# Two causal masking routes, a bias fold in four steps, and a packed ring of exponentials

## The reference

```
xn1 = ln(x, g1, be1)
q, k, v = xn1 @ Wq_s + bq_s, xn1 @ Wk_s + bk_s, xn1 @ Wv_s + bv_s     # 16 heads of 32
scores = where(tril, q @ k.T * sqrt(32), -inf)                      # causal
x = x + softmax(scores) @ v @ W1 + b1
xn2 = ln(x, g2, be2)
x = x + softmax((xn2 @ Wq_c + bq_c) @ kc.T * sqrt(32)) @ vc @ W2 + b2    # over the context
x = x + relu(ln(x, g3, be3) @ Wf1 + bf1) @ Wf2 + bf2
```

## Time and profile before

| | |
|---|---|
| median of three runs | 2273.32 us |
| the profiled execution | 2272.72 us |
| its span | 2270.9 us |
| busy PE, PEld | 2161.4, 1604.5 us |
| busy DVE, ACT, POOL | 1395.7, 868.7, 932.4 us |
| scores of causal attention end | about 966 us into the span |

### The profile page before, as it was taken

How to read it: one execution, slowest core, us unless ns; L and a number is a source line. 1 busy time by engine, 2 the same in 40 slices (tenths; PEclk the granted TensorE clock), 3 DMA queues, 4 the chain that set the end, 5 groups by cost and what they waited for, 6 DMA issues and landing times.

```text
span 2270.9 us, 32174 instructions
## 1 busy us (share of the span) xinstructions
PE 2161.4 (95%) x11590; PEld 1604.5 (71%) x11590; DVE 1395.7 (61%) x3349; ACT 868.7 (38%) x1610; POOL 932.4 (41%) x943
## 2 busy tenths in 40 slices
PE   7999999999999998889999998999999999999996
PEld 5666666666656664467777776888887887888784
DVE  5577766876786676456666677543455636455546
ACT  4156555655565555534333433221221222121213
POOL 1068767777777778643333342101020202111112
PEclk9999999999999997999999999999999999999998
DMA  7655555555564564211122121320112121121101
GB/s 234 78 82 97 93 85 87 106 89 83 91 111 76 82 96 126 71 56 56 56 70 77 63 80 42 121 84 24 61 61 82 53 74 66 65 66 56 42 33 47
DMA packets 106324, 177.34 MB, mean 78 GB/s; under 512 B 18335, under 2 KB 23455, under 8 KB 106161
## 3 DMA queue, kind: packets, MB, share of 16 engines
q1 hardware_dynamic: 106164, 175.29, 33.1%
HBM read 83.67 MB, written 40.13 MB: 55 GB/s over the span
## 4 chain that ended last, share of the span: by engine, by line
PE 81%; DVE 7%; ACT 5%; issue 3%; POOL 2%; DMA 1%; SPq 0%; POOLq 0%; ACTq 0%; DVEq 0%
PE psum L55 19%; PE psum L56 18%; PE psum L57 18%; PE psum L821 6%; PE psum L766 6%; PE psum L809 5%; PE psum L724 1%; DVE psum L1027 1%; ACT sx L1377 1%; PE psum L830 1%; PE psum L743 1%; PE psum L1327 1%; DMA small<-es 1%; PE psum L1319 1%; PE psum L1268 1%
## 5 line engine op out<-in xcount | busy, mean ns | idle before, releaser
L681 POOL TENSOR_TENSOR es<-es,er 128x512 f32<-128x512 f32 (+3 forms) x640 | 588.0, 959 | 258.4 <-PE psum L821 243.6
L922 ACT ACTIVATE er<-psum 128x512 f32<-128x512 f32 (+3 forms) x640 | 278.4, 471 | 285.6 <-DVE psum L1038 176.2
L1027 DVE CUSTOM_DVE_ANT_0 psum<-psum,mask_ts 128x384 f32<-128x384 f32 (+3 forms) x512 | 249.4, 502 | 152.9 <-PE psum L766 150.6
L766 PE MATMUL psum<-ks,qs 96*128 96x512 f32 (+3 forms) x768 | 260.4, 371 | 7.4 <-DVE mx L1027 3.5
L809 PE MATMUL psum<-qs,ks 100*128 100x512 f32 (+3 forms) x768 | 252.0, 365 | 10.6 <-DVE mx L1027 5.1
L1876 ACT ACTIVATE fy<-psum,cols 128x512 f32<-128x512 f32 x128 | 88.2, 689 | 451.9 <-PE psum L57 451.4
L766 PEld LDWEIGHTS psum<-ks,qs 96*128 96x128 f32 x768 | 139.7, 191 | 115.2 <-issue 32.9
L1031 DVE TENSOR_REDUCE mx<-psum 128x1 fp32r<-128x512 f32 x256 | 175.6, 686 | 61.0 <-PE psum L766 60.0
L55 PE MATMUL psum<-fh,hh 128*128 128x512 f32 x512 | 201.0, 393 | 7.1 <-DVE hl L1977 7.1
L55 PE MATMUL psum<-fah,fh 128*128 128x512 f32 x512 | 202.9, 396 | 0.0
L1975 DVE CAST hh<-fy 128x512 fp32r<-128x512 f32 x128 | 61.2, 478 | 228.5 <-ACT fy L1876 228.1
(11 more groups left out here) (260 smaller groups left out, 4588.7 us busy)
## 6 DMA issues: line engine op xcount, KB each, us to landing
qs<-stage SPq DMA_DIRECT2D x96, 256.0 KB, 5.7
ks<-stage SPq DMA_DIRECT2D x96, 256.0 KB, 8.3
rs<-rs_d SPq DMA_DIRECT2D x32, 256.0 KB
sa_d<-rs SPq DMA_DIRECT2D x32, 256.0 KB, 2.1
sx<-sa_d SPq DMA_DIRECT2D x8, 1024.0 KB, 5.7
xt<-in_x SPq DMA_DIRECT2D x32, 256.0 KB, 6.0
x_d<-xt SPq DMA_DIRECT2D x32, 256.0 KB, 2.0
fw<-in_Wf SPq DMA_DIRECT2D x16, 512.0 KB, 5.3
```

The costliest lines, as they stand in the source:

```text
L681: e.tensor_tensor(es, es, er, ALU.add).then_inc(s_add.sem, 1)
L766: t = e.matmul(bank1(*s)[:, v * wd:v * wd + wd], Q.qs[par][0:96, i, 128 * ti:128 * ti + 128], Q.ks[par][0:96, i, c0:c0 + wd], start=True, ...
L922: e.activation(dst, bank1("sc", g, c2, j, i)[:, off:512], ACT.Exp, scale=SCALE).then_inc(s_freeS.sem, 1)
L1027: t = e.tensor_tensor_reduce(out=ps, in0=ps, in1=mask_ts[:, 512 - wd:512], scale=1.0, scalar=-3e38, op0=ALU.add, op1=ALU.max, accum_out=mx ...
```

## The change

Four things. The list of planned times is first rewritten as tables with a row for each of the first four, the middle eight (one row for each of four) and the last four groups; the numbers in them are those of before, but for the transfers `stack` of group 1, which come 0.07 later in the list. Then:

- **Masks of group 14.** Its 32 diagonal scores have no `low` step. TensorE follows each with a second matmul into the same bank, the identity times a copy of the mask. The copy is made once, on ScalarE (`mkr`, planned 13.78), over a weight tile that is used no more; the W2 split waits until group 14's scores are through, since it shares the memory. `ex` of these scores stands 0.001 behind its score in the list and no longer 0.028, and the banks of 124 steps around it change.
- **Bias fold.** `2wb` becomes four steps at 14.983, 15.023, 15.063 and 15.103; the work is the same.
- **Ring.** `er` is one strip of 4096 columns; each score takes its true width, and waits for the latest of those that lay there.

```diff
+MASKED_BY_PE = (14,)
-                if s[0] == "sc" and s[3] >= 4 * c2 :
+                if s[0] == "sc" and s[3] >= 4 * c2 and g not in MASKED_BY_PE:
                     t += [(a + 0.014, ("low", *s[1:])), (a + 0.028, ("ex", *s[1:]))]
+    t.append((MASKED_BY_PE[0] - 0.22, ("mkr",)))
+CROSS_FOLD = 0.04
+    t = [(CROSS_ONCE[2] + CROSS_FOLD * m, ("2wb", m)) for m in range(4)]
+        for at, (g, c2, j, i) in Q.slot_of.items():
+            width = 512 - max(0, 128 * (j - 4 * c2))
+            pos = 0 if pos + width > 4096 else pos
+            under = [n for n, (lo, hi) in held.items() if lo < pos + width and pos < hi]
+            Q.freed_by[at] = max(under, default=None)
+            for n in under:
+                lo, hi = held.pop(n)
+                if hi > pos + width:
+                    held[n] = pos + width, hi
+            Q.piece[at] = slice(pos, pos + width)
+            pos += width
+            held[at] = Q.piece[at].start, pos
+        def mask_r():
+            return Q.W["v"][0][:, 0, 0:128]
+                    diag = g in MASKED_BY_PE and j >= 4 * c2
                     t = e.matmul(ps[:, off:512], Q.ks[par][0:100, i, 128 * j:128 * j + 128],
-                                 Q.qs[par][0:100, i, 512 * c2 + off:512 * c2 + 512], start=True, stop=True)
+                                 Q.qs[par][0:100, i, 512 * c2 + off:512 * c2 + 512], start=True, stop=not diag)
+                    if diag:
+                        w.wait_ge(s_mkr, 1)
+                        t = e.matmul(ps[:, off:off + 128], identr[:], mask_r(), start=False, stop=True)
+                elif s[0] == "mkr":
+                    w.wait_ge(s_const, 6)
+                    w.wait_ge(s_fillA, Q.useA["vm", 7, 3] + 1)
+                    e.activation(mask_r(), mask_st[:], ACT.Copy).then_inc(s_mkr.sem, 1)
-                        dst = Q.er[:, at % 8, off:512]
-                        if at >= 8:
-                            w.wait_ge(s_add, at - 7)
-                            w.wait_ge(s_pv, Q.pv[Q.slot_of[at - 8]] + 1)
+                        dst, last = exps(at), Q.freed_by[at]
+                        if last is not None:
+                            w.wait_ge(s_add, last + 1)
+                            w.wait_ge(s_pv, Q.pv[Q.slot_of[last]] + 1)
-                for m in range(4):
-                    for k in range(KT):
+                m = s[1]
+                for k in range(KT):
+                if m == 3:
+                    t.then_inc(s_fillK.sem, 1)
+                if j == 2:
+                    w.wait_ge(s_fillS, read(MASKED_BY_PE[-1], 1, 1))
```

More of the change, by code:

```diff
@@ L119, in attn_steps, with row @@
     yield ("none",), 200
-LN_LOAD = (-2.514, -2.024, -1.712, -1.56)
-LN_TURN = (-2.071, -1.822, -1.573, -1.348)
-CUT = (0.292, 0.27, 0.283, 0.294)
+LN_LOAD = ((-2.514, -2.024, -1.712, -1.56), (-2.514, -2.024, -1.712, -1.56), (-2.514, -2.024, -1.712, -1.56))
+LN_TURN = ((-2.071, -1.822, -1.573, -1.348), (-2.071, -1.822, -1.573, -1.348), (-2.071, -1.822, -1.573, -1.348))
+CUT = (0.292, 0.27, 0.283, 0.294, 0.292, 0.27, 0.283, 0.294, 0.292, 0.27, 0.283, 0.294)
 PROJ_0 = (27.2, 31.3, 37.9, 40.4)
-PROJ_1 = (-1.329, -1.236, -1.109, -1.047)
-PROJ = ((-1.661, -1.491, -1.269, -1.082), (-1.853, -1.456, -1.346, -1.171), (-1.872, -1.647, -1.316, -1.202), (-1.958, -1.475, -1.34, -1.21))
-PROJ_LONG = (0.067, 0.08, 0.146, 0.146)
+PROJ = ((-1.661, -1.491, -1.269, -1.082), (-1.329, -1.236, -1.109, -1.047), (-1.872, -1.647, -1.316, -1.202), (-1.958, -1.475, -1.34, -1.21), (-1.661, -1.491, -1.269, -1.082), (-1.853, -1.456, -1.346, -1.171), (-1.872, -1.647, -1.316, -1.202), (-1.958, -1.475, -1.34, -1.21), (-1.661, -1.491, -1.269, -1.082), (-1.853, -1.456, -1.346, -1.171), (-1.872, -1.647, -1.316, -1.202), (-1.958, -1.475, -1.34, -1.21))
+PROJ_LONG = (0.05, 0.05, 0.146, 0.146, 0.067, 0.08, 0.146, 0.146, 0.067, 0.08, 0.146, 0.146)
 VALUES_0 = (40.2, 52.3, 66.7, 68.9)
-VALUES = ((-1.149, -0.992, -0.719, -0.081), (-1.444, -1.08, -0.796, -0.377))
+VALUES = ((-1.149, -0.992, -0.719, -0.081), (-1.444, -1.08, -0.796, -0.377), (-1.149, -0.992, -0.719, -0.081), (-1.444, -1.08, -0.796, -0.377), (-1.149, -0.992, -0.719, -0.081), (-1.444, -1.08, -0.796, -0.377))
 VALUES_LONG = 0.1
 MAX_0 = -0.007
-MAX_1 = (-0.809, -0.507, -0.024)
-MAX = ((-1.031, -0.726, -0.051), (-1.012, -0.739, -0.002), (-1.033, -0.705, -0.043), (-0.988, -0.72, -0.05))
+MAX = ((-1.031, -0.726, -0.051), (-0.809, -0.507, -0.024), (-1.033, -0.705, -0.043), (-0.988, -0.72, -0.05), (-1.031, -0.726, -0.051), (-1.012, -0.739, -0.002), (-1.033, -0.705, -0.043), (-0.988, -0.72, -0.05), (-1.031, -0.726, -0.051), (-1.012, -0.739, -0.002), (-1.033, -0.705, -0.043), (-0.988, -0.72, -0.05))
+def row(g, n=4):
+    return g if g < n else n + g % n if g < 3 * n else g - n
+MASKED_BY_PE = (14,)
 def order1():
@@ L158, in order1 @@
         for qt in range(4):
-            t += ln_times(b, qt, 4 * b + LN_LOAD[qt], 4 * b + LN_TURN[qt])
+            t += ln_times(b, qt, 4 * b + LN_LOAD[b - 1][qt], 4 * b + LN_TURN[b - 1][qt])
     for g in range(16):
-        r = g % 4
+        r = row(g)
         cut = CUT[r]
-        at = [at0(a) for a in PROJ_0] if g == 0 else [g + a for a in (PROJ_1 if g == 1 else PROJ[r])]
+        at = [at0(a) for a in PROJ_0] if g == 0 else [g + a for a in PROJ[r]]
         for c2 in range(2):
@@ L166, in order1 @@
                 n = 2 * c2 + wq
-                t += proj_times(g, c2, wq, at[n], at[n] + (0.05 if g < 2 else PROJ_LONG[r]))
-                back = g - 2 + (CUT[(g - 2) % 4] if n == 0 else CUT[(g - 2) % 4] + (1 - CUT[(g - 2) % 4]) * 0.54 if n == 1 else 1) + 0.03
-                t.append((at[n] + 0.1 if g == 0 else max(at[n] + PROJ_LONG[r] + 0.07, back), ("stack", g, c2, wq)))
+                t += proj_times(g, c2, wq, at[n], at[n] + PROJ_LONG[r])
+                past = CUT[row(g - 2)] if g >= 2 else 0.3
+                back = g - 2 + (past, past + (1 - past) * 0.54, 1, 1)[n] + 0.03
+                t.append((at[n] + 0.1 if g == 0 else max(at[n] + (0.22 if g == 1 else PROJ_LONG[r] + 0.07), back), ("stack", g, c2, wq)))
         if g % 2 == 0:
             for sp in range(4):
-                s, d = (at0(VALUES_0[sp]), 0.05) if g == 0 else (g + VALUES[r // 2][sp], VALUES_LONG)
+                s, d = (at0(VALUES_0[sp]), 0.05) if g == 0 else (g + VALUES[row(g // 2, 2)][sp], VALUES_LONG)
                 t += spread(s, s + d, [(("vm", g // 2, sp, i), 1) for i in range(4)])
                 t.append((s + d, ("ve", g // 2, sp)))
-        m0, m1, end = (at0(46), at0(54), MAX_0) if g == 0 else [g + a for a in (MAX_1 if g == 1 else MAX[r])]
+        m0, m1, end = (at0(46), at0(54), MAX_0) if g == 0 else [g + a for a in MAX[r]]
         t += spread(m0, m1, max_steps(g, 0)) + spread(m1, end, max_steps(g, 1))
@@ L438, in program @@
         O1 = [s for _, s in O1]
-        Q.useA, Q.useP, Q.useM, Q.useS, Q.outS, Q.slot, Q.pv = {}, {}, {}, {}, {}, {}, {}
+        Q.useA, Q.useP, Q.useM, Q.useS, Q.outS, Q.slot, Q.pv, Q.low = {}, {}, {}, {}, {}, {}, {}, {}
         for s in O1:
@@ L452, in program @@
                 Q.slot[s[1:]] = len(Q.slot)
+            if s[0] == "low":
+                Q.low[s[1:]] = len(Q.low)
             if s[0] == "pv":
@@ L456, in program @@
         Q.slot_of = {at: k for k, at in Q.slot.items()}
+        Q.piece, Q.freed_by, held, pos = {}, {}, {}, 0
+        for at, (g, c2, j, i) in Q.slot_of.items():
[10 more added lines that the diff above has]
+            held[at] = Q.piece[at].start, pos
         d_rows, d_ct0, d_wv0, d_wt0, d_wg0, d_out0 = (sem(n) for n in ("d_rows", "d_ct0", "d_wv0", "d_wt0", "d_wg0", "d_out0"))
@@ L474, in program @@
         s_sao, s_rcp, s_rec, s_low = sem("s_sao"), sem("s_rcp"), sem("s_rec"), sem("s_low")
+        s_mkr = sem("s_mkr")
         def stk(par, w, c2):
@@ L537, in x_rows, with exps @@
             return Q.xr[:, i, :] if b else Q.v[:, 2 * qt + i, :]
+        def mask_r():
+            return Q.W["v"][0][:, 0, 0:128]
+        def exps(at):
+            return Q.er[:].rearrange("p a n -> p (a n)")[:, Q.piece[at]]
         def raw1(j):
@@ L674, in pool1 @@
                         at = Q.slot[g, c2, j, i]
-                        es, er = Q.esum[c2][i][:, off:512], Q.er[:, at % 8, off:512]
+                        es, er = Q.esum[c2][i][:, off:512], exps(at)
                         if j == 1:
@@ L818, in pe1 @@
                         w.wait_ge(s_sao, 2 * g + c2)
-                        src = Q.er[:, Q.slot[g, c2, j, i] % 8, :] if j else Q.esum[c2][i][:]
+                        src = exps(Q.slot[g, c2, j, i]) if j else Q.esum[c2][i][:]
                         h = 128 * (g % 2) + 32 * i
-                        e.matmul(bank[BO][32 * i:32 * i + 32, off:512], values(g)[:, j, h:h + 32], src[:, off:512],
+                        e.matmul(bank[BO][32 * i:32 * i + 32, off:512], values(g)[:, j, h:h + 32], src,
                                  start=j == 0, stop=j == nj - 1).then_inc(s_pv.sem, 1)
@@ L903, in act1 @@
```

(18 more changed lines are left out.)

2 lines of the change are left out of this document (1 added, 1 removed).

## The result

| | median | runs | lowest to highest |
|---|---|---|---|
| before | 2272.66 us | 6 | 2270.26 to 2276.59 |
| after | 2280.22 us | 6 | 2278.92 to 2282.14 |

The ratio is 1.0033 (95% interval 1.002 to 1.0046): the change costs 7.6 us. I had forecast 2269.0, with a range to 2278, and given "slower" a chance of 0.09. The profiled execution took 2279.31 us, its span 2277.5, which is 6.6 over the span of before.

A forecast was written before the change was run, and what follows sets the result against it. The prediction took TensorE, busy 95% of the span, to bound the kernel. From 2272.7 us, half 0 (0), half 1 (-2), fold (-1.5) and ring (0) gave 2269.2, predicted as 2269, range 2260 to 2278.

The forecast's parts named there:

- slower: Whole kernel: a time above 2280.1 us, given a chance of 0.09.
- no engine held TensorE up from 896 to 909: Bias fold after group 14: TensorE busy all 13 us, so letting scores through in between saves nothing by itself.
- the term of -2 for half 1: Diagonal blocks of half 1, group 14: banks return sooner without VectorE's mask additions; -2 us, ends -4.2 and +4.2.
- the three rivals: Other outcomes: the clock holds, 2261 us (0.22); TensorE pays, 2281 (0.13); gains hidden anyway, 2273 (0.13).
- a low clock and the masks' price: Group 14 onward: low clock lasts past the last fold step, masks cost 0.26 us each; +8.2, 2281 us, chance 0.13.
- Price of a mask: Each mask matmul on TensorE: 0.11 us at full clock, 0.22 at half; ends 0.11 and 0.26.
- Half 0: 0: Half 0 of group 14, 16 masks: what follows waits for a gather's DMA, so 0 us, ends -1 and +1.
- rival (a): Group 14 from 877 us: masks and earlier banks keep the clock up; 2261 us in all, chance 0.22.
- Fold: -1.5: Bias fold in four steps: same work, but the clock can come back sooner; -1.5 us, ends -6.4 and +2.2.
- 2bw: 0: VectorE's `2bw` between third and fourth fold step: VectorE waits up to 1.7 us for TensorE; 0, end +1.
- Ring: 0: Packed ring of exponentials: tightest one in group 14 has 0.7 us of room; 0 us, ends -2 and +2.
- scores of group 15 begin later: Sign that the forecast is wrong; it expected the group-15 scores to start some 2 us earlier.

The follow-up runs named there:

- scalar_half1: The kernel after with the eight copies on ScalarE and VectorE adding the masks of half 0 of group 14 again: 2266.94 us.
- copies_on_scalar: The kernel after with the eight context-tile copies (`2cd`) moved from VectorE to ScalarE: 2265.61 us.
- before_scalar: The kernel before with only the eight copies moved from VectorE to ScalarE: 2273.84 us.
- scalar_fold_whole: The kernel after with the eight copies on ScalarE and the bias fold in one piece again: 2264.49 us.
- scalar_ring8: The kernel after with the eight copies on ScalarE and the ring of exponentials back at eight full-width places: 2270.38 us.
- fold_and_ring: The kernel after without masks on TensorE (VectorE adds them); fold in four steps, packed ring and copies on VectorE stay: 2276.12 us.
- copies_as_sums: The kernel after with VectorE's eight copies written as `tensor_reduce` sums over an axis of length one: 2265.57 us.

## Why the prediction was wrong

**The step that failed** is the sentence in the part on the fold that no engine held TensorE up from 896 to 909, and with it the term of -2 for half 1, which counted what VectorE loses and not what those additions did for the order. TensorE was busy there, but the fold covered a wait for VectorE's queue. For masks and ring I had -2 in all and the runs show +2.5; for the fold I had -1.5 and they show +4.7. I read VectorE's queue as far as the maxima and the splits. I did not see that the eight copies in it took 3.19 us where eight times 0.28 is 2.2, that one of them took 1.78, and that it ended with a pause of GpSimd. That pause hung on a mask addition that I was about to remove. None of the three rivals had it; "slower" was there only by a low clock and the masks' price.

**Price of a mask.** As forecast: scores of 128 columns and masks follow each other 0.11 us apart at full clock (888.03, 888.14, 888.25). Its half-clock value hardly mattered, since the clock was at 0.96.

**Half 0: 0.** Right, and for the reason given: the gather still ended it. The reciprocal that waits for it came at the same place as in the earlier trace rows, with the idle time changed from 2.08 to 1.16. scalar_half1, 1.3 us over copies_on_scalar, is within the noise of it.

```profile
861.10 0.25 DVE L1090 RECIPROCAL small<-small 128x16 f32<-128x16 f32 x1 [1.16 <-DMA small<-es]
```

**Half 1: -2.** Too small where the copies are free, mainly by the mechanism of rival (a), a clock that stays up. With the copies on ScalarE, masks and ring together bring 9.3 us (2273.8 to 2264.5). The stretches from 877 and 896, in before_scalar and then in scalar_fold_whole, with the columns of the earlier trace rows:

```profile
877.00:896.00 19.00, 17.31 (x58) 7.04 (x51) 13.40 (x36) 12.18 (x26) 19.00 (x18) 0.64 0.32 110
896.00:909.00 13.00, 11.88 (x60) 9.97 (x59) 3.37 (x11) 6.47 (x18) 12.30 (x11) 0.50 0.34 103
```

```profile
877.00:896.00 19.00, 17.75 (x120) 12.02 (x120) 11.00 (x25) 15.87 (x38) 19.00 (x19) 0.94 0.22 79
896.00:909.00 13.00, 12.45 (x59) 6.47 (x61) 6.01 (x21) 7.99 (x19) 13.00 (x12) 0.83 0.28 85
```

Of the 9.3 us, 4.8 hang on the packed ring, by scalar_ring8 beside copies_on_scalar. Rival (a) had -11.3. I had given it 0.22, and its "against" (861 to 877 is not changed) was no hindrance. But the masks' place alone does not settle the clock: fold_and_ring, with the masks on VectorE, has 0.91 from 877 to 896, and copies_as_sums, with the masks on TensorE, fell to half from about 879 to 882. After itself had the gain in group 14 too: it is the 7.7 us named above. The microsecond from 877 had 0.15 us of matmuls and ended at a falling clock; in after it has 0.37 at a clock of 1.00:

```profile
877.00:878.00 1.00, 0.37 (x3) 0.17 (x2) 0.72 (x3) 1.00 (x3) 1.00 (x2) 1.00 0.28 107
```

**Fold: -1.5.** Wrong in sign. The steps took about what I said, 0.8 or 1.7 us (1.05 and 0.95 at full clock, 1.70 at half), but I compared them only by the clock and not by what the one piece covered: a wait for VectorE in either kernel. Two steps of 1.70 us now stand behind the 14.7 us wait, and the clock, at half since TensorE idled, stays low through them: 0.85 from 909 to 973, against 0.92. Nor does the fold always run at half clock: in scalar_fold_whole the one piece took 3.75 us at full clock, and the clock fell as it ended (0.81 in the microsecond from 893).

**2bw: 0.** VectorE waited 4.00 us for the last fold step, where I had up to 1.7, and `2bw` came at 915.01; no run isolates it.

**Ring: 0.** Right for the kernel before (2272.6), wrong in company: with the masks on TensorE and the ring of eight, the exponentials wait 3.0 us for the sums and the kernel is 4.8 us slower. I had 0.7 us of room for the tightest one at the old pace, and did not work it out again at the new.

**The sum.** By runs: masks and ring +2.5 (2275.5 against 2273.0), fold in four +4.7, together +7.2, which is after against the 2273.0 of that round; against the 2272.7 of the first table it is 7.6. Without the held copies the same two are -9.3 and +1.1 from 2273.8, the latter within the noise. The parts don't add up across the two tables: what each is worth depends on the wait next to it.

What I had written down as a sign of error was "scores of group 15 begin later". They began earlier, and the kernel was slower: the first ones tell of group 14, and the second pair, 16 us behind them, of the queue on VectorE.

## What to carry to other kernels

When a step is removed from an engine, look at what is left in its queue and at what the removed wait gave to others: a pause of a third engine can be what lets a neighbour run. When a group of equal instructions has a longest one far above its median and no wait recorded (15.8 us against 0.28 here), look for what stopped on another engine as it ended. Work that stands in front of a wait can be free, as the fold was, so don't cut it up before the wait is gone. The version of after with the copies written as sums, or on ScalarE, is the one to keep: 2265.6 us either way, and for the sums a ratio of 0.9967 (0.9954 to 0.998) to before.

## What the runs showed of the hardware

- One VectorE copy of 128x256 between two SBUF tiles lasted 15.82 us instead of 0.28, across more than ten GpSimd instructions in a row (sums that read two tiles, and two memsets that only write), and ended 0.15 us after GpSimd had stopped. The Trainium skill, "SBUF — State Buffer", section "SBUF: two separate sides", has the ports held for one whole instruction; here the ends of single GpSimd instructions did not let the copy in, only a pause did. What the shortest such pause is was not tried: the shortest ones seen are 1.69 and 2.23 us.
- From 874 to 889 us, beside the same unbroken GpSimd run, VectorE's splits, which read a bank and a tile (0.68 us), and its maxima over a bank (0.69 us) ran at their usual length.
- The same move by `tensor_reduce` over an axis of one costs 0.41 us against 0.28, and was not held beside the same GpSimd run.
- The granted clock differs between executions of one kernel, and the time with it: of the six of copies_as_sums the two slowest took 2268.1 us at a mean clock of 0.986 and 0.987, the two fastest 2261.6 and 2261.8 us at 0.991.
